# The weight products of two convolutions: one dense matmul of 216 columns a block, put in order when VectorE reads PSUM

## What is computed

```python
coarse_up = jax.image.resize(coarse, (B, H, W, Cc), 'bilinear')
attn = jax.nn.sigmoid(conv1x1(jnp.mean(fine, axis=(1, 2), keepdims=True), attend_w))
fine_cal = conv1x1(fine * (attn + 1.0), select_w)
align = conv1x1(jnp.concatenate([fine_cal, coarse_up * 2.0], axis=-1), offset_w)
om = conv3x3_same(align, om_w, om_b)
n_off = DG * 2 * K * K
off = om[..., :n_off].reshape(B, H, W, DG, K * K, 2)
mask = jax.nn.sigmoid(om[..., n_off:]).reshape(B, H, W, DG, K * K)
aligned = dcn_v2(coarse_up, off, mask, dcn_w, dcn_b)
return jax.nn.relu(aligned) + fine_cal
```

## Time and profile before

| | |
|---|---|
| median of 3 runs | 3370.52 us (3359.72 to 3374.48) |
| the profiled execution | 3370.08 us |
| its span, first to last instruction | 3368.4 us |
| PE busy | 3117.9 us, 93% |
| DVE busy | 2515.5 us, 75% |
| ACT busy | 1517.4 us, 45% |
| granted TensorE clock, mean | 0.967 |

### The profile page before, as it was taken

The page is one execution under the profiler, slowest core; times in us unless marked ns, Lnnn a source line. Parts: engine busy times, 40 slices in busy tenths (PEclk is TensorE's granted clock), DMA queues, the critical chain, the costliest instruction groups (busy, mean ns, idle before and its releaser), DMA issues.

```text
span 3368.4 us, 91473 instructions
## 1 busy us (share of the span) xinstructions
PE 3117.9 (93%) x34242; PEld 2697.5 (80%) x34242; DVE 2515.5 (75%) x4215; ACT 1517.4 (45%) x2787; POOL 335.5 (10%) x445
## 2 busy tenths in 40 slices
PE   8969999999999938999998999998999998999999
PEld 7859999989999827878776777777777786877788
DVE  3427888888888859878776877887787786878782
ACT  0012222222222116656655565665666565656663
POOL 2000000000000001111111111111111111111111
PEclk9979999999999969999999999999999999999999
DMA  5322344333333232322223222223222233322222
GB/s 165 100 88 73 58 69 71 60 47 52 61 58 55 30 60 43 62 58 61 55 62 58 60 54 64 63 53 68 53 60 54 61 65 55 64 55 61 54 62 57
DMA packets 452882, 211.30 MB, mean 63 GB/s; under 512 B 230821, under 2 KB 447541, under 8 KB 452277
## 3 DMA queue, kind: packets, MB, share of 16 engines
q1 hardware_dynamic: 426112, 161.74, 26.6%
q10 hardware_dynamic: 21724, 26.37, 2.4%
q0 software_dynamic: 4608, 16.78, 1.3%
HBM read 104.86 MB, written 55.23 MB: 48 GB/s over the span
## 4 chain that ended last, share of the span: by engine, by line
PE 48%; ACT 7%; issue 6%; DVE 2%; ACTq 1%; SPq 1%; DMA 0%; POOL 0%; DVEq 0%; POOLq 0%
PE eb L1555 26%; PE tb L1113 14%; PE vb L1135 6%; ACT taps_all L1084 2%; ACT res L1142 1%; ACT wtT L1118 1%; ACT om L1040 1%; PE eb L1148 1%; PE tb L1035 1%; ACTq L1006 1%; DVE wt L1107 1%; ACT mask L1049 1%; ACT ot L1153 0%; SPq L1030 0%; ACTq L1435 0%
## 5 line engine op out<-in xcount | busy, mean ns | idle before, releaser
L1555 PE MATMUL eb<-val,wd 128*128 128x256 f32 (+1 forms) x4680 | 1225.7, 385 | 0.0
L1118 ACT COPY wtT<-tb 128x512 f32<-128x512 f32 x1152 | 662.7, 587 | 682.2 <-PE tb L1113 680.8
L1555 PEld LDWEIGHTS eb<-val,wd 128*128 128x128 f32 x4680 | 798.4, 191 | 120.8 <-issue 57.4
L1113 PE MATMUL tb<-ident,wt 128*128 128x128 f32 x4608 | 710.2, 278 | 85.7 <-issue 37.0
L1113 PEld LDWEIGHTS tb<-ident,wt 128*128 128x128 f32 x4608 | 564.7, 143 | 239.6 <-issue 77.1
L1107 DVE TENSOR_TENSOR wt<-taps_all 128x768 f32<-128x768 f32 x768 | 731.4, 994 | 10.4 <-PE tb L1113 2.1
L547 PE MATMUL conv<-fine,wf 128*108 128x256 f32 x4608 | 593.5, 290 | 13.1 <-DVE omT L878 13.1
L547 PEld LDWEIGHTS conv<-fine,wf 128*108 128x108 f32 x4608 | 572.8, 174 | 28.7 <-issue 28.7
L1488 DVE COPY val<-vb 128x432 f32<-128x432 f32 (+1 forms) x384 | 212.7, 554 | 240.4 <-PE vb L1135 240.1
L1135 PE MATMUL vb<-wtT,win 64*32 64x144 f32 x16384 | 323.3, 292 | 60.7 <-issue 56.4
L1135 PEld LDWEIGHTS vb<-wtT,win 64*32 64x32 f32 x16384 | 245.6, 108 | 108.5 <-issue 108.0
(11 more groups left out here) (142 smaller groups left out, 2499.8 us busy)
## 6 DMA issues: line engine op xcount, KB each, us to landing
val<-val SPq DMA_DIRECT2D x128, 396.0 KB, 3.8
win<-cpad SPq DMA_DIRECT2D x304, 64.0 KB
om_s<-om_d SPq DMA_DIRECT2D x1152, 12.0 KB
chunk<-in_x SPq DMA_DIRECT2D x32, 512.0 KB, 5.0
xchunk<-in_x SPq DMA_DIRECT2D x32, 512.0 KB, 4.1
r_d<-r POOLq DMA_DIRECT2D x32, 512.0 KB, 3.2
rt<-r_d SPq DMA_DIRECT2D x63, 256.0 KB, 4.9
out<-ot ACTq DMA_DIRECT2D x63, 256.0 KB, 2.9
```

The lines of the kernel that those rows point to most:

```text
L1113: last = nc.tensor.transpose(tb[b][:, 128 * j:128 * j + 128], wt[half][:, 4 * i + j, :], ident[:])
L1118: return nc.scalar.copy(dst, src) if e == "act" else nc.vector.tensor_copy(dst, src)
L1555: done = nc.tensor.matmul(eb[q][:, 256 * fo:256 * fo + rows], wd[:, half, k, 128 * fo:128 * fo + 128], val[:, half, k, at:at + rows // W, ...
```

## The change

`merge` now has one matmul for each block m: all 216 columns, in the order in which they lie in `om_w`, into 216 adjacent columns of the bank. `split` brings them into the order by tap: both of its steps become two instructions, one for the shifts (144 columns) and one for the masks (72), which read PSUM with steps of 18 and 9 floats and write runs of 16 and 8 floats. `w_hi` counts both first parts, `merged_out` is signalled by the last instruction.

```diff
             rows, taps, _, _ = products[n]
-            by_tap = wps[n % 2][:, 0:NOM].rearrange("p (k c) -> p k c", k=NK)
             for m in range(NT):
-                nc.tensor.matmul(by_tap[:, :, 0:2 * NG].rearrange("p k (t g) -> p k t g", t=2), owT[:, m, rows, :],
-                                 taps[:, m, 0:2 * GK].rearrange("p (g k t) -> p k t g", g=NG, k=NK),
-                                 start=(m == 0), stop=False)
-                last = nc.tensor.matmul(by_tap[:, :, 2 * NG:TAPC], owT[:, m, rows, :],
-                                        taps[:, m, 2 * GK:NOM].rearrange("p (g k) -> p k g", g=NG),
-                                        start=False, stop=(m == NT - 1))
+                last = nc.tensor.matmul(wps[n % 2][:, 0:NOM], owT[:, m, rows, :], taps[:, m, :], start=(m == 0), stop=(m == NT - 1))
             last.then_inc(merged, 1)
...
                 dve.wait_ge(merged, n + 1)
-                made = wps[n % 2][:, 0:NOM]
-                nc.vector.tensor_scalar(parts[0], made, factor, None, ALU.mult).then_inc(w_hi, 1)
-                dve.wait_ge(w_hi, n + 1)
-                nc.vector.scalar_tensor_tensor(out=parts[1], in0=made, scalar=factor, in1=parts[0].bitcast(f32),
-                                               op0=ALU.mult, op1=ALU.subtract).then_inc(merged_out, 1)
+                made = wps[n % 2]
+                shifts = made[:, 0:2 * GK].rearrange("p (g k t) -> p k t g", g=NG, k=NK)
+                masks = made[:, 2 * GK:NOM].rearrange("p (g k) -> p k g", g=NG)
+                by_tap = [t.rearrange("p (k c) -> p k c", k=NK) for t in parts]
+                hi, lo = ((t[:, :, 0:2 * NG].rearrange("p k (t g) -> p k t g", t=2), t[:, :, 2 * NG:TAPC]) for t in by_tap)
+                for to, part in zip(hi, (shifts, masks)):
+                    nc.vector.tensor_scalar(to, part, factor, None, ALU.mult).then_inc(w_hi, 1)
+                dve.wait_ge(w_hi, 2 * n + 2)
+                for to, near, part in zip(lo, hi, (shifts, masks)):
+                    last = nc.vector.scalar_tensor_tensor(out=to, in0=part, scalar=factor, in1=near.bitcast(f32),
+                                                          op0=ALU.mult, op1=ALU.subtract)
+                last.then_inc(merged_out, 1)
```

## The result

The changed kernel takes 3215.95 us (median of 4 runs, 3213.65 to 3219.29) beside 3369.99 us before (4 runs, 3359.72 to 3374.48): the ratio is 0.955, 95% interval 0.952 to 0.957. That is 154 us less. I had forecast 61 less (3309 us) and a range of 3298 to 3322: the direction is right, the size is not, and the time lies far under the range.

A forecast was written before the change was run, and what follows sets the result against it. Stage 1 was taken as bound by PE's merge matmuls; seven rounds, 7 x (21.99 - 13.1) = 62.2 us, less 1.5 at the start gave 61, so 3370 - 61 = 3309 us, range 3298 to 3322.

The forecast's parts named there:

- PE's gain per product: Stage 1 merges on PE: dense 216-column records take 0.183 us each, a product 1.47 us instead of 3.00.
- the first rival: Stage 1 merges: column order is not what slows them, a product takes 2.98 us, nothing changes, 3369 us; 4%.
- The lower clock at the start: Start of stage 1: 1.5 us of the gain is not had.
- DVE's read-out: Stage 1, DVE reading each product from PSUM: 0.94 us against 0.80, plus 0.19 for jumping reads (0 to 0.39).
- The rivals through DVE: Stage 1, costly jumping PSUM reads: 3318 us (13%), DVE becoming the bound 3341 (4%), or slower 3395 (3%).
- The second one: Stage 1: jumping PSUM reads cost 1.5 ns per column above dense, read-out 1.57 us, total 3318 us; 13%.
- The round: Stage 1, six products plus turning and counting four chunks of x: 13.1 us instead of 21.99, seven times.
- The 0.06 us for the signal: Stage 1: assumed delay from DVE finishing a read-out to PE starting the next product in that bank.
- What else is touched: Outside the merges: x loads stay hidden, later stages just start earlier, so the whole 61 us gain is kept.
- What would show it: Signs: right if records are 0.183 us apart and batches 13.1; wrong if 0.37, or a later stage is longer.

The follow-up runs named there:

- the two halves above: Kernel before with only dense merge results, operand still stepped: 3380.56 us; kernel before with only dense operands, results jumping in PSUM: 3322.23 us (3364.92 before both).
- the eight padded kernels: Changed kernel plus tiny unread PE matmuls at the end of stage 1, adding 32, 64, 128, 160, 176, 192, 208 or 256 instructions: 3209.22 to 3372.09 us.
- padding of 128, 160 and 176: Changed kernel with that many PE instructions added as tiny unread matmuls at the end of stage 1: 3295.84, 3305.36 and 3372.09 us.

## Why the prediction was right and wrong

- *PE's gain per product.* Right: 0.183 us a record and 1.46 a product. The reason held too: the first rival (the order is not what slows the merge) is refuted by the two halves above, and they show that it is the read side of the order.
- *The lower clock at the start.* No run shows the sum's term of 1.5 us by itself. What the changed kernel shows: granted 0.52 from 25 to 30 us; dense records start 0.36 us apart from 25.14 to 29.82 and 0.183 from 30.02 on; the first product's read-out starts at 27.91, 3.29 us after PE's first matmul, where the later pace (1.47 and 0.22 for the answer) would give 1.7. Seven rounds of 9.15 us less would be 64.0; 62.4 were saved, so the start kept 1.6 of the gain.
- *DVE's read-out.* The jumping PSUM read, for which I took 0.19 us a product of a possible 0.39, costs nothing: 0.305 and 0.223 us for 144 and 72 columns, where dense rows had 0.309 and 0.227. The nearest control is the kernel with the stepped operand and the dense result above: there DVE runs the same four instructions but reads PSUM without jumps, with a mean of 308 and 223 ns:

```profile
L231 DVE TENSOR_SCALAR wf<-wps 128x144 fp32r<-128x144 f32 x24 | 7.4, 308 | 47.0 <-PE wps L157 47.0
```

The rivals through DVE had no ground. (The second one's read-out is 1.59 us by its own terms, not 1.57, which changes nothing.) The pair of reads, 144 and then 72 columns, takes 0.45 us where 0.305 + 0.223 would be 0.53: the second starts before the first has ended.

- *The round.* Forecast 13.1, or 12.92 with free jumps; measured 12.84. Stage 1 gained 62.4 us for the 61 (62 with free jumps) of the sum. The 0.06 us for the signal was an assumption; in stage 1 before, DVE's first copy of `owT` ends at 8.99 and PE's first weight load behind it starts at 9.04, 0.05 us later.
- *The failed step* is the last one of "What else is touched": "the later stages just start earlier". I took the code behind the change as unmoved because no instruction of it changed. It moved by 672 instructions, which is 160 within the blocks of 256, and q8's nine packets a pass in stage 3 went to none: 99.3 us over the 63 strips. Putting it back brought 344 packets and 3305 us; giving it to the kernel before, 94 packets and 3277 us. Nothing in the sum stood for that, and no rival either; "What would show it" named only a later stage that gets longer. That the 62 us of stage 1 came as forecast is not luck, but the time of the whole was wrong by the part that had no term.

It could have been seen. The page gives 346 instruction packets of 16384 bytes, 88,576 instructions, for a list of about 21,000 instructions on PE (by their records, an fp32 matmul is four, a transpose two); that many can only come from loops that are fetched again, and the strips of 30.4 and 34 us in turn, with waits for "issue" inside a run of matmuls, mark the loop. That the change shortens PE's list by a number that is no multiple of 256 stands in the order of the instructions.

The loop need not be fetched in every pass: in the changed kernel it ran some 28 passes, from 1365 to 3114 us, without a packet on q8, so its 1709 instructions, 6.7 blocks, can all stay. And in the slow kernels PE's short waits stand in the middle of the loop, before the matmuls of lines 1113 and 1135 in the timeline of the kernel before.

The 5.4 us that stage 2 and the start of stage 3 took longer need no cause. From the last counting batch to the first copy it is 1056.2 us before and 1061.7 after, and in the eight padded kernels with the same stage 1 as the changed one it lies anywhere from 1056.1 to 1060.2.

Left open: the exact rule for which places stay (padding of 128, 160 and 176 does not, the six others tried do), since where PE's list starts in a block is not known. A slow pass has nine packets, one more than the blocks that 1709 instructions can lie over; what the ninth is for is not shown.

## What to carry to other kernels

Before forecasting an edit, look at the page's instruction packets and at the loops: when a loop is fetched anew in each pass, or nearly is, an edit ahead of it moves it and can give or take more than the edit itself (here 99 us beside 62). So measure an edit with padding that keeps the remainder by 256 instructions, and try a few paddings on the finished kernel. A short stop of PE can also cost clock behind it (here stops of 2.13 and 1.81 us, then 6.8 us at 0.50): compare the granted clock before calling a difference a wait. Lay out what PE reads as the moving operand densely and put any reordering on the output: in these forms that cost nothing on PE when it was done in the write to PSUM (0.47 us a block, as dense), and only the extra instructions when it was done in DVE's read of PSUM (0.305 us for 144 columns, 0.308 without jumps).

## What the runs showed of the hardware

- In stage 1 of the kernel before, one packet of 16384 bytes comes on q8 for each round of 256 PE records. Instructions added to PE's list alone moved the packets of q8 (91 to 344 with 160 more, 92 with 256 more); q14's stayed 92.
- With the loop of 1709 PE instructions moved within blocks of 256, the runs had 344 to 346 packets on q8 (nine a pass) or 91 to 101, and the former took 83 to 162 us more over 63 strips. In the kernel before, PE's 45 short stops between 1400 and 3100 us end 2.24 to 3.09 us after a packet has started.
- Two stops of 2.13 and 1.81 us with 1.1 us of work between them were followed by 6.8 us at a granted clock of 0.50; stops of 2.37 and 0.84 us with 2 us between them were not.
- An fp32 moving operand read with steps of 18 or 9 floats takes 1.72 to 1.75 ns a column at full clock, a dense one 0.83 to 0.85 (0.183 us for 216).
- Neither single-float jumps of a matmul's result in PSUM (0.47 us a block, as dense) nor DVE's single-float jumps when it reads PSUM (0.305 us for 144 columns, 0.308 without jumps) cost anything. In PSUM, read with jumps, 144 and 72 columns differ by (0.305 - 0.223) / 72 = 1.14 ns a column.
- Tiny fp32 matmuls (32 x 32 weights, one column) run at 0.033 us a record on PE: 80 of them in 2.69 us, hidden in the wait for DVE.

```profile
116.38 2.69 PE L179 MATMUL small<-ident 32*32 32x1 f32 x80
```
